# A graph network's segment softmax: TensorE and ScalarE bring some chunks' running sums into row order instead of VectorE

## The reference

```
msg = relu(z[src] + e) + 1e-7          # e = edge_attr @ w + b, the same in all layers
m = msg * t
seg_max = segment_max(m, dst)
ex = exp(m - seg_max[dst])
denom = segment_sum(ex, dst)
agg = segment_sum(msg * ex / denom[dst], dst)
out = z + agg
h = h + relu(layernorm(out @ w1 + b1)) @ w2 + b2
z = relu(layernorm(h))                 # input of the next layer
```

## Time and profile before

| | |
|---|---|
| median of 3 runs | 4217.13 us |
| lowest and highest | 4204.82 and 4222.44 us |
| the profiled execution's own time | 4254.22 us |
| its span | 4252.4 us |
| mean granted TensorE clock | 0.778 |
| busy: PE, DVE, ACT, POOL | 70%, 65%, 39%, 60% |

### The profile page before, as it was taken

One profiled execution on the slowest core, in us unless ns is written; L12 is line 12 of the kernel. 1 busy time (PEld: TensorE's weight loads), 2 busy tenths in 40 slices (PEclk: granted clock), 3 DMA queues, 4 the chain that ended last, 5 costly groups with the idle time before them and its releaser, 6 DMA issues.

```text
span 4252.4 us, 48618 instructions
## 1 busy us (share of the span) xinstructions
PE 2955.6 (70%) x18494; PEld 1343.3 (32%) x18494; DVE 2769.2 (65%) x2608; ACT 1652.7 (39%) x2251; POOL 2537.0 (60%) x2651
## 2 busy tenths in 40 slices
PE   4766676776367777777657777777756777777774
PEld 2323232333223333333333333333323333333333
DVE  4766687777646666666765666666673666666668
ACT  1544453344423333333433333333343333333345
POOL 5665665655365565665565556666655655565655
PEclk7877787778577887887767877778867888877886
DMA  5787787887547777777656777777763777777764
GB/s 165 211 221 194 217 216 199 202 217 188 144 150 197 194 205 204 202 201 197 146 157 174 200 189 202 208 198 203 203 146 124 208 200 196 194 204 200 205 165 83
DMA packets 1041513, 800.46 MB, mean 188 GB/s; under 512 B 913146, under 2 KB 934655, under 8 KB 1015616
## 3 DMA queue, kind: packets, MB, share of 16 engines
q1 hardware_dynamic: 934480, 454.32, 46.3%
q10 hardware_dynamic: 23776, 246.29, 16.2%
q0 software_dynamic: 83024, 96.75, 9.3%
HBM read 498.09 MB, written 299.01 MB: 187 GB/s over the span
## 4 chain that ended last, share of the span: by engine, by line
PE 54%; issue 24%; DVE 12%; another core or an unknown queue 5%; ACT 4%; POOL 1%; SPq 1%; DMA 0%; DVEq 0%; POOLq 0%; ACTq 0%
PE X L643 44%; PE X L624 5%; PE X L653 3%; DVE decay L1008 3%; DVE state_all L1023 2%; DVE X L1013 1%; DVE rows_all L994 1%; DVE one_hot L1110 1%; ACT X L766 1%; DVE state_all L1039 1%; ACT msg L764 1%; DVE x_sb L1101 1%; POOL between L552 1%; PE X L677 0%
## 5 line engine op out<-in xcount | busy, mean ns | idle before, releaser
L525 POOL DMA_INDIRECT gath<-z_table,idx x2432 | 2352.0, 967 | 1526.1 <-issue 726.2
L643 PE MATMUL X<-one_hot,z_parts 128*64 128x512 fp8e5 x9450 | 1490.6, 434 | 669.2 <-issue 521.5
L643 PEld LDWEIGHTS X<-one_hot,z_parts 128*64 128x64 bf16 x9450 | 654.9, 122 | 1532.8 <-issue 1060.1
L643 PE MATMUL X<-between,z_parts 128*64 128x512 fp8e5 x5400 | 844.2, 425 | 309.5 <-issue 297.0
L1006 DVE TENSOR_TENSOR decay<-decay,top 128x1 f32<-128x1 f32 x216 | 34.2, 158 | 1329.3 <-ACT X L766 1255.8
L764 ACT ACTIVATE msg<-X,edge_bias 128x1024 f32<-128x1024 f32 (+2 forms) x216 | 228.5, 1058 | 1619.0 <-remote 1123.9
L643 PEld LDWEIGHTS X<-between,z_parts 128*64 128x64 bf16 x5400 | 371.9, 119 | 788.3 <-issue 606.7
L776 ACT ACTIVATE decay<-X 128x1024 f32<-128x1024 f32 (+2 forms) x216 | 209.3, 969 | 855.4 <-issue 515.1
L994 DVE STREAM_TRANSPOSE rows_all<-state_all 128x1024 f32<-128x1024 f32 (+3 forms) x432 | 505.7, 1171 | 9.6 <-DMA rows_table<-rows_all 2.1
L1008 DVE TENSOR_TENSOR_SCAN decay<-X,decay 128x1023 f32<-128x1023 f32 (+2 forms) x216 | 477.2, 2209 | 7.7
L1023 DVE TENSOR_TENSOR_SCAN state_all<-decay,state_all,X 128x1024 f32<-128x1024 f32 (+2 forms) x216 | 468.2, 2167 | 20.0 <-issue 10.7
(11 more groups left out here) (180 smaller groups left out, 1218.8 us busy)
## 6 DMA issues: line engine op xcount, KB each, us to landing
rows_table<-rows_all SPq DMA_DIRECT2D x784, 256.0 KB
attr<-attr_t SPq DMA_DIRECT2D x196, 512.0 KB
one_hot<-one_hot_dram ACTq DMA_DIRECT2D x39, 1920.0 KB
between<-one_hot_dram ACTq DMA_DIRECT2D x36, 1920.0 KB
one_hot<-one_hot_dram ACTq DMA_DIRECT2D x39, 1280.0 KB
one_hot_dram<-one_hot SPq DMA_DIRECT2D x25, 1920.0 KB
between<-one_hot_dram ACTq DMA_DIRECT2D x36, 1280.0 KB
gath<-z_table,idx POOLq DMA_INDIRECT x2432
```

The source lines that it names most:

```text
L525: pool.indirect_dma_start(out=gath[s][:, n * F:(n + 1) * F], out_offset=None, in_=z_table, in_offset=bass.IndirectOffsetOnAxis(ap=idx[:, c ...
L643: last = nc.tensor.matmul(x[h * F:(h + 1) * F, BANK:CH], z_parts[:, i * GB + k, third, :], bank[:, k, i, h * BANK:(h + 1) * BANK], start=F ...
```

## The change

In layer 0 the states of the odd chunks from 3 to 47 (those have no one-hot product), and in all layers those of the last five chunks, are no longer turned by VectorE. TensorE turns them in tiles of 128x128 into the chunk's own tile X, which is free once its numerator sums are done, and ScalarE copies them from there to the rows tile: denominators first, then numerators (`copy_rows`). In layer 0 TensorE turns the denominators of chunk c - 2 behind the rows of the odd chunk c, does one of the three one-hot pieces of part 1, waits for ScalarE's copy, turns the numerators, and then does the last two pieces. The edge product of chunk c + 2, which uses the same X, moves to behind the rows of chunk c + 1. ScalarE's copies stand behind the messages of chunk c. The rows of such a chunk lie otherwise in the rows tile, and its stores write 1 KB for each partition and tile, where the others write pieces of 256 B. The stores of the padding behind the last chunk of layer 0 become a DMA of their own. `rows_ready` becomes two semaphores.

```diff
+def turned_by_pe(layer, c):
+    return c > LAST_FULL or layer == 0 and c % 2 == 1 and 3 <= c
...
+def row_place(c):
+    return 0 if c <= LAST_FULL + 2 else 1536 if c == NCH - 1 else 1024
...
+    def stored_rows(c, n, part):
+        p0 = part * SQ
+        row = STARTS[c] * HALVES
+        return rows_table[row:row + n * P * HALVES, :].rearrange("(k p h) e -> p k (h e)", p=P, h=HALVES)[p0:p0 + SQ]
...
-                sp.wait_ge(rows_ready, g + 1)
+                sp.wait_ge(rows_ready[g % 2], g // 2 + 1)
+                if turned_by_pe(layer, c):
+                    k, k0 = n * SQ // P, row_place(c) // (HALVES * 2 * F)
+                    for a in parts:
+                        sp.dma_start(stored_rows(c, k, a), rows_by_tile[g % 2][a * SQ:(a + 1) * SQ, k0:k0 + k, :]).then_inc(stored[g % 2], 16)
+                    return
...
+            def turn_piece(layer, c, q, at):
+                g = layer * NCH + c
+                for k in range(tiles(c)):
+                    last = nc.tensor.transpose(X[g % XS][:, at + k * P:at + (k + 1) * P], state[g % 2][:, q, k * P:(k + 1) * P],
+                                               ident[:, :])
+                last.then_inc(pieces_turned, 1)
...
                     add_rows(layer, c)
+                    if c == LAST_FULL + 3:
+                        turn_rows(layer, c - 2)
                     if layer > 0 and c + 1 in chosen(layer):
                         add_by_one_hot(layer, c + 1, 1)
-                    if c + 2 < NCH:
+                    if layer == 0 and c % 2 == 0 and turned_by_pe(layer, c - 3) and c <= LAST_FULL + 2:
+                        edge_product(layer, c + 1)
+                    if c + 2 < NCH - 1 and not (layer == 0 and turned_by_pe(layer, c - 2) and c <= LAST_FULL + 1):
                         edge_product(layer, c + 2)
-                    if layer == 0 and c + 1 in chosen(layer):
+                    if c == NCH - 2:
+                        edge_product(layer, NCH - 1)
+                    if layer == 0 and turned_by_pe(layer, c - 2) and c <= LAST_FULL + 1:
+                        pe.wait_ge(num_ready, c - 1)
+                        turn_piece(layer, c - 2, 0, 0)
+                        if c + 1 in chosen(layer):
+                            add_by_one_hot(layer, c + 1, 1, but_last=2)
+                        pe.wait_ge(den_copied, turned_up_to(layer, c - 2))
+                        turn_piece(layer, c - 2, 1, 0)
+                        if c + 1 in chosen(layer):
+                            add_by_one_hot(layer, c + 1, 1, only_last=2)
+                    elif layer == 0 and c + 1 in chosen(layer):
                         add_by_one_hot(layer, c + 1, 1)
...
+            def copy_rows(layer, c):
+                g = layer * NCH + c
+                w, late = width(c), turned_up_to(layer, c)
+                act.wait_ge(stored[g % 2], STORES_PER_LAYER[g % 2] * layer + 16 * NSTORE * (c // 2 - (c > LAST_FULL + 2) - (c == NCH - 1)))
+                at, den_at = row_place(c), BANK if w <= BANK else 0
+                to = rows_all[:, g % 2].rearrange("p b q j -> p (b q j)")[:, at:at + 2 * w].rearrange("p (m q j) -> p m q j", q=2, j=SQ)
+                act.wait_ge(pieces_turned, 2 * late - 1)
+                nc.scalar.activation(to[:, :, 0, :], X[g % XS][:, den_at:den_at + w].rearrange("p (m j) -> p m j", j=SQ), ACT.Copy)\
+                    .then_inc(den_copied, 1)
+                act.wait_ge(pieces_turned, 2 * late)
+                act.wait_ge(den_copied, late)
+                nc.scalar.activation(to[:, :, 1, :], X[g % XS][:, 0:w].rearrange("p (m j) -> p m j", j=SQ), ACT.Copy)\
+                    .then_inc(rows_ready[g % 2], 1)
...
                     messages(layer, c)
+                    if layer == 0 and turned_by_pe(layer, c - 2) and c <= LAST_FULL + 1:
+                        copy_rows(layer, c - 2)
+                    if LAST_FULL < c - 3:
+                        copy_rows(layer, c - 3)
...
                 nc.scalar.activation(ends_exp[:, :], ends_shift[:, :], ACT.Exp).then_inc(ends_exped, 1)
+                copy_rows(layer, NCH - 3)
+                copy_rows(layer, NCH - 2)
+                copy_rows(layer, NCH - 1)
...
-                if g >= 2:
-                    dve.wait_ge(stored[g % 2], STORES_PER_LAYER[g % 2] * layer + 16 * NSTORE * (c // 2))
-                turn_state(layer, c, 0, den_turned)
+                if not turned_by_pe(layer, c):
+                    if g >= 2:
+                        dve.wait_ge(stored[g % 2], STORES_PER_LAYER[g % 2] * layer + 16 * NSTORE * (c // 2))
+                    turn_state(layer, c, 0, den_turned)
```

More of the change, by code:

```diff
@@ L78, in tiles, with turned_up_to @@
     return width(c) // P
+def turned_by_pe(layer, c):
+    return c > LAST_FULL or layer == 0 and c % 2 == 1 and 3 <= c
+def turned_up_to(layer, c):
+    return sum(turned_by_pe(k, m) for k in range(layer + 1) for m in range(NCH) if k < layer or m <= c)
+def row_place(c):
+    return 0 if c <= LAST_FULL + 2 else 1536 if c == NCH - 1 else 1024
 def first_tile(c):
@@ L211, in gnn_kernel @@
         rows = [rows_all[:, s] for s in range(2)]
+        rows_by_tile = [rows_all[:, s].rearrange("p b q j -> p (b q j)").rearrange("p (k e) -> p k e", e=HALVES * 2 * F) for s in range(2)]
         below = state_all[:, :, :, :].rearrange("p a b c -> p (a b c)")[:, 0:NT * P].rearrange("p (t r) -> p t r", r=P)
@@ L390, in store_rows @@
                 b0 = at // SQ
-                n = NSQ - b0 if layer == 0 and c == NCH - 1 else width(c) // SQ
-                sp.wait_ge(rows_ready, g + 1)
+                n = width(c) // SQ
+                sp.wait_ge(rows_ready[g % 2], g // 2 + 1)
[4 more added lines that the diff above has]
+                    return
                 for a in parts:
@@ L463, in _ @@
                         sp.dma_start(x_sb[:, :, :], x_nodes).then_inc(nodes_landed, 16)
+                    if layer == 0 and c == NCH - 1:
+                        past = rows_table[COLS * HALVES:BOUNDARY_ROW, :].rearrange("(k p h) e -> p k (h e)", p=P, h=HALVES)
+                        sp.dma_start(past, rows_by_tile[1][:, 0:NBLK * KT - COLS // P, :]).then_inc(zero_stored, 16)
                     store_rows(layer, c, range(NSTORE if c < NCH - 1 else NSTORE // 2))
@@ L534, in _ @@
                 if layer == 0:
-                    pool.wait_ge(zero_stored, 16)
+                    pool.wait_ge(zero_stored, 32)
                     pool.wait_ge(pos_ready, 1)
@@ L620, in edge_product @@
                     pe.wait_ge(num_ready, g - XS + 1)
+                if c >= XS and turned_by_pe(layer, c - XS):
+                    pe.wait_ge(rows_ready[g % 2], (g - XS) // 2 + 1)
                 w = min(width(c), BANK)
@@ L626, in edge_product, with add_by_one_hot @@
                 last.then_inc(attr_used, 1)
-            def add_by_one_hot(layer, c, part):
+            def add_by_one_hot(layer, c, part, but_last=0, only_last=GB):
                 x = X[(layer * NCH + c) % XS]
@@ L636, in add_by_one_hot @@
                     pe.wait_ge(hot_landed[hot_slot(c)][part], 16 * (loads_before(layer, c) + 1))
-                for k in range(*PARTS[part]):
+                a, b = PARTS[part]
+                for k in range(max(a, b - only_last), b - but_last):
                     if layer == 0:
@@ L656, in add_rows, with turn_rows @@
                 last.then_inc(x_ready, 1)
+            def turn_rows(layer, c):
+                g = layer * NCH + c
+                for q, ready in enumerate((den_ready, num_ready)):
+                    pe.wait_ge(ready, g + 1)
+                    turn_piece(layer, c, q, BANK if q == 0 else 0)
+            def turn_piece(layer, c, q, at):
[4 more added lines that the diff above has]
+                last.then_inc(pieces_turned, 1)
             def turn_z(q, i, n):
@@ L726, in _ @@
                 last.then_inc(ends_t, 1)
+                turn_rows(layer, NCH - 1)
                 pe.wait_ge(ends_ready, layer + 1)
+                for k in (g - 1, g):
+                    pe.wait_ge(rows_ready[k % 2], k // 2 + 1)
                 if layer == 0:
```

25 lines of the change are left out of this document (15 added, 10 removed).

## The result

The changed kernel takes **4347.67 us** (median of 4, 4341.58 to 4355.25), the one before 4210.98 (4203.14 to 4222.44) on the same chip: **1.0306 times** as long, 95% interval 1.0278 to 1.0334. Forecast were 4254, in 4160 to 4310. The profiled execution took 4344.19 us (span 4342.4), the profiled one of before 4254.22: 90 us more, though the medians differ by 137.

A forecast was written before the change was run, and what follows sets the result against it. No engine's busy share was named the bound; layer 0's chunk pairs wait on TensorE's releases, the tails on VectorE. Layer 0's 31 us, tails 2 and a mask load 4 make 37, so 4217 becomes 4254 us, range 4160 to 4310.

The forecast's parts named there:

- between them ScalarE waits for TensorE's second turn: ScalarE's two copies per odd chunk, layer 0: the wait between them is the turn's own 1.1 to 2.2 us.
- VectorE's idle 7 to 10 us a pair covers it: Layer 0, each even and odd chunk: VectorE's next start, 0.8 to 1.9 us later, is hidden by its idle time.
- the denominator scan waits less than 1 us for exponents: Sign to check: VectorE's denominator scan would wait under 1 us for ScalarE's exponents.
- The messages of the even chunk: Sign in layer 0: they follow the odd chunk's messages by 15 to 17 us, where it was 13.
- short pair: Even and odd chunk of layer 0 taking 37.3 us together; 12 of the 23 were taken to be so.
- The 60 matmuls: Layer 0's last 60 one-hot matmuls wait for the denominator's copy and end 1.5 to 3.9 us later; 1.9 taken.
- short pairs turn long: Rival: the last 60 matmuls fall inside the next gathers, all layer 0 pairs take 44.9 us; +90, 4313 us; chance 0.16.
- The mask load: Layer 0, behind the late stores: the even chunk's mask pass waits 2 to 4 us; 0.7 added for each of 12 pairs.
- The tails: Last five chunks of each layer, VectorE the bound: -4.9 to +3 us a layer; +0.5 taken, times four 2 us.
- less work on VectorE wins little: Layer 0: 57 us of transposes leave VectorE, but at most 15 us is won, 0.67 a chunk.
- I move the median by the same 37: Total: the terms' 37 us, from the profiled execution, added to the median of 4217 give 4254 us.
- long pairs: Even and odd chunks of layer 0 taking 44.9 us together; 11 of the 23 were taken to be so.

The follow-up runs named there:

- copies_early_masks: Changed kernel, but TensorE turns nothing in layer 0, ScalarE still copies from PSUM, mask load ahead of odd chunk's stores: 1.0023 times before on chip III.
- tails_only: Changed kernel, but VectorE turns layer 0's odd chunks as before; TensorE turns only each layer's last five chunks: 1.0044 times before on chip II.
- before_again: The kernel before, unchanged, profiled again on chip III: 3451 us.

## Why the prediction was wrong

**The step that failed** is the one on ScalarE's work: "between them ScalarE waits for TensorE's second turn", priced at the turn's own 1.1 to 2.2 us. The turn is that short where nothing is in its way (1.04 and 1.09 us above), but the hand-off took 6.4 us in the mean, and the first, priced at nothing, 2.6. Two things were left out. On chips with late signals, a signal of TensorE can come as late as the x_ready that the prediction had itself read in the earlier trace rows; it was not asked of the new signals. And the second turn stands behind 30 one-hot matmuls that wait for VectorE. The second, with the turn itself, makes 4.4 to 4.5 us of the 6.4: so much is left on chip III and in both kernels without gathers, where no signal is late. The first makes, by the difference, the other 1.9 and the 2.6 ahead of the first copy. What each costs in time depends on the cover: with the gathers running and the signals prompt (chip III) layer 0 loses 8 us (764.7 to 772.9), against 75 on chip I; without gathers 53 and 62, late masks included. No run parts the 75 us of chip I between the two.

**The cover.** "VectorE's idle 7 to 10 us a pair covers it": right for a delay of 2 us, and the layer 0 stage of copies_early_masks, 8 us under before's on chip III, shows it. It was spent at waits of up to 21.3 us. What is late next was named right: exponents, then the next scan. The sign that failed is "the denominator scan waits less than 1 us for exponents": 190.7 us in 23 pairs. The messages of the even chunk followed those of the odd one by 24.0 us in the mean, with 17.8 before, where 15 to 17 were forecast for a short pair.

**The 60 matmuls** ("I take +1.9 for a short pair"): no run shows a cost of this wait of its own. The rival "short pairs turn long" had the effect and the price: 7 pairs more are over 41 us, and 4313 was its time, 96 over the median then known; the profiled execution rose by 90. That is luck in part, for its cause was another: in chunk 21 the last 60 matmuls run in one burst of 9.39 us from 579.85, behind the gathers (to 576.3) and not inside them, and what is late is the hand-off ahead of them. Its 4313 also lies outside the forecast's range of 4160 to 4310, though it had a chance of 0.16.

**The mask load**, 0.7 us for 12 pairs: each wait was right (2 to 4 us; measured 66.5 / 22 = 3.0), but it comes in nearly every pair. Taking it away is worth 18 us on chip III; on chip IV nothing that can be told, as the hand-offs cover it.

**The end of layer 0** cost 7.3 us at a place that the forecast didn't name. GpSimd reads 14 values (needed, L566) behind its wait for zero_stored. That wait now takes in a store that SyncE issues only at 1185.42, so the reads moved from GpSimd's idle time to the path (first the kernel before, then after; the start of the first and the last is at the end):

```profile
L539 POOLq TENSOR_LOAD <-enough x14: 282/808/1162, 1073.2 to 1085.3; - x14
```

```profile
L566 POOLq TENSOR_LOAD <-enough x14: 282/288/512, 1189.2 to 1196.6; - x14
```

From 1189.2 to 1197.1 is 7.9 us. No run moved them alone, so this is read, not tested. On chip III the end of layer 0 grows by more, from 99.2 us to between 107.9 and 109.3 in every changed kernel, and is the largest term left there. The tails themselves: chunks 48 to 53 of layers 1 to 3 take 38.0 us after and 37.0 before, +1.0 a layer for a forecast of +0.5, inside its bounds.

**Right were** the counts (392 to 346 transposes, 56.7 us for 57), the copies (1.01 and 1.02 us for 1.1) and that less work on VectorE wins little (8 us of the stage in copies_early_masks). The eight transposes took 1.09 us for 1.10 where they ran in one go. The Trainium skill ("TensorE: Matmul & The Clock Gate", Part 4) would have 2.2 by its 275 ns each, an estimate, and here too the rows show half. The 1 KB stores ran at 0.21 MB a us with the DMA engines 99.0% busy, against 0.16 in the earlier trace rows: faster by a third, and no run shows what that is worth.

**The baseline.** "I move the median by the same 37" took the difference between two profiled executions for that between the medians. Before's profiled execution stands 43 us above its median, the one of after 3 below: 47 us of the miss of 94. (The terms of the sum make 53, 90 for 37; the median of before, 4211 for the 4217 then known, takes 6 off.) On chip II tails_only, with VectorE turning layer 0, had 893.2 us there, 38.8 a pair and all but one under 43. I take it, and no run shows it, that the trace of before has some 6 long pairs (43 / 7.6) more than usual; executions without a profile have no trace.

**Still open:** why TensorE's signals come late with the gathers on chips I, II, IV and V and not on III; the share of late masks on a chip with late signals once the hand-offs are gone (copies_early_masks ran only on chip III); and the after kernel on chip II.

No version here beats the kernel before.

## What to carry to other kernels

Price a hand-off between engines by what its signal took at that place in the trace, not by the length of the work that it signals; when a trace shows one engine's signals 10 us late in some stretch, ask it of every new dependency that is put there (here, by the difference between chips I and III, it held the two hand-offs for 2.6 and 1.9 us a chunk in the mean). Count too what stands on the queue ahead of the work that signals: here 30 matmuls, which with the turn made 4.4 us. An idle share covers a delay only as long as the delay is small against one gap. When a wait is widened (here zero_stored), look at what stands behind it on that engine.

## What the runs showed of the hardware

Chip III ran the kernel before in 3451 us, the other Trainium2 chips in 4211 to 4320. On these TensorE's signals can arrive some 10 us late while GpSimd gathers (78 of 176 in the trace of before came over 2 us late, none of 243 in that of before_again on chip III), those of ScalarE (0 of 188) and VectorE (2 of 305) hardly ever do. In some stretches of the gathers TensorE also issues only one instruction in about 1.2 us (eight transposes start from 570.51 to 579.16), though eight others ran in 1.09 us at 550.89, in the same run of gathers. Without gathers the same stage takes 704 and 697 us on both sorts. The granted clock was 0.78 and 0.83 in layer 0, too little for that difference. A change that lengthens a chain of hand-offs cost 3% on the one sort and 0.9% on the other.
